# Queries and keys first in the projection, and the setup of a fused transformer block in another order

## The chip, the cores and the metric

One core of a Trainium2 chip runs the whole kernel in one launch. The metric is the device time of a launch in microseconds. TensorE (PE in the profile) multiplies matrices, VectorE (DVE), ScalarE (ACT) and GpSimd (POOL) do the elementwise work, and SyncE (SP) issues most of the DMAs. Each engine works through its own list of instructions in order and meets the others only in semaphores.

## The reference, cut to what matters

```python
mod = silu(condition) @ Wada + bada                       # (8, 6*512)
sh_a, sc_a, gt_a, sh_m, sc_m, gt_m = split(mod, 6)
xm = layernorm(x, g1, be1) * (1 + sc_a) + sh_a            # x is (8, 1024, 512), f32
q, k, v = heads(xm @ Wqkv)                                # 16 heads of 32
attn = softmax(causal(q @ k.T * 32**-0.5))
x = x + gt_a * ((attn @ v) @ Wproj + bproj)
xm = layernorm(x, g2, be2) * (1 + sc_m) + sh_m
x = x + gt_m * (gelu(xm @ W1 + b1) @ W2 + b2)             # hidden width 2048
```

## The kernel before, in words

Products with weights are made from a high and a low part of each operand (three matmuls for one), so each weight and each activation is split: ScalarE or VectorE rounds it to the high part, VectorE or GpSimd subtracts to get the low part.

**The projection** (Wqkv) runs over 16 blocks of 512 rows of x. A block (`ia`) is normalised on VectorE (`ln_stats`, `ln_aggregate`, `normalise`, the power on GpSimd), turned by four PE transposes (`a_turn`), given scale and shift on ScalarE (`a_modulate`), split on VectorE (`a_split`, one column part k at a time) and then multiplied in 12 items (`a_item`) of 12 matmuls each. Items 0 to 3 are the values of 128 rows each, items 4 to 7 the queries of a group of four heads, items 8 to 11 the keys. ScalarE copies each item out of PSUM (`a_copy`); a value item goes to DRAM from ScalarE's own queue (`v_store`); a query or key item is split by a cast on VectorE (`a_high`) and a subtraction on GpSimd (`a_low`), and SyncE stores it (`a_store`).

**Attention** runs over 32 pairs of batch and head group, two in each of 16 bodies of 40 steps. In each step PE makes scores, ScalarE takes their exponentials, GpSimd masks and adds, and PE multiplies by the values. A row's largest score is found beforehand: nine pieces for each pair (`max_item`), each some wide matmuls into psS (line 745), on VectorE a mask where the piece meets the diagonal (line 1223) and a reduction (line 1227). PE may begin piece n only when piece n-1 has been reduced, since both lie in psS. `max_join`, `max_turn` and `max_row` make a row of the results, and `place_max` sets it beside the queries.

**What runs ahead.** Blocks 0, 1 and 2 are projected in the setup, before body 0 (AHEAD = 3); body u projects block u+3 in its steps by the written table `A_SHARES`, and works on the largest scores of later pairs by `MAX_AT`. The setup has the nine pieces of pair 0 behind items 1 to 9 of block 2; the pieces of pair 1 stand in body 0, the first six in its first six steps (`MAX_FIRST_AT`). Where a step ends an item, the step after has its `a_high`, the next its `a_store`.

**The start.** The modulation is made from silu(condition) and six parts of Wada of 1 MB each: parts 0 and 1 ahead of block 0, parts 2 to 5 between blocks 0 and 1. Each part is four fp32 matmuls of eight output rows by 512 columns (line 672), all into PSUM partitions 0 to 7, followed by four small transposes (line 679). VectorE makes the coefficients from them (lines 1153, 1156). Wqkv is loaded and split in four row parts of 128x1536; VectorE makes the low parts of two of them (line 1136), GpSimd those of the other two, and item 0 needs all four.

**The end of attention.** Behind the last body SyncE issues the loads of six of the eight parts of W2, then waits for the stores of the attention's output and only then issues `load_x_gate(1)`, which brings gate, biases and x rows for block 1 of the MLP, and after it the attended rows of block 2.

The whole order is written out by hand; no planner moves anything.

## Time and profile before

| | us |
|---|---|
| median of three runs | 3336.97 (3336.56 to 3337.72) |
| profiled execution, its own time | 3334.65 |
| its span | 3332.9 |
| PE busy | 3207.0 |
| DVE busy | 2081.0 |
| POOL busy | 1549.8 |
| ACT busy | 1175.2 |
| mean granted clock of TensorE | 0.993 |

The span is what the profile covers; the execution's own time is 1.75 us more. Busy times of the engines overlap, so they don't add to the span. Times in the rows below count from the span's start. From there on the setup ends and body 0 begins at 176, attention ends near 1683, and the MLP takes the rest.

### The profile page before, as it was taken

The numbers are of one execution on the slowest core, as the hardware profiler recorded it, in microseconds if no ns is written. First come the engines' busy times: TensorE is split into PE (matmuls) and PEld (weight loads), VectorE is DVE, ScalarE is ACT, GpSimd is POOL, SyncE is SP. The second block draws the span as 40 slices with busy tenths as digits, with TensorE's granted clock in tenths as the row PEclk, the third lists the DMA queues.
The fourth block names the chain that finished last, engine by engine and source line by source line (L and its number), as shares of the span: only waits on it lengthen the run. The fifth ranks groups of instructions, "written<-read, shape, count | busy, mean of one in ns | idle before, by whom it ended". The sixth has DMA issues, their size and how long they took to land.

```text
span 3332.9 us, 70516 instructions
## 1 busy us (share of the span) xinstructions
PE 3207.0 (96%) x25708; PEld 2575.1 (77%) x25708; DVE 2081.0 (62%) x2511; ACT 1175.2 (35%) x2330; POOL 1549.8 (47%) x1304
## 2 busy tenths in 40 slices
PE   7989999999999999998889999999999999999999
PEld 4656666666666666665578898898988989889888
DVE  5567777677777767667665555555555555555552
ACT  2245555555555555555531121211211212112111
POOL 2246666666666666677762332333333333323232
PEclk9989999999999999999999999999999999999999
DMA  5546656656565665566632222222122222222220
GB/s 216 186 131 176 184 169 172 180 166 176 176 184 168 172 180 167 163 191 170 153 108 61 71 53 60 72 57 60 53 63 72 53 60 69 60 60 53 60 63 13
DMA packets 303514, 391.88 MB, mean 118 GB/s; under 512 B 24240, under 2 KB 206000, under 8 KB 303336
## 3 DMA queue, kind: packets, MB, share of 16 engines
q1 hardware_dynamic: 292080, 372.04, 39.6%
q10 hardware_dynamic: 11264, 17.31, 1.5%
q8 instruction: 140, 2.29, 0.3%
q14 instruction: 30, 0.25, 0.0%
HBM read 270.66 MB, written 118.06 MB: 117 GB/s over the span
## 4 chain that ended last, share of the span: by engine, by line
PE 85%; DVE 8%; issue 3%; ACT 2%; DMA 1%; SPq 0%; DVEq 0%; POOL 0%; ACTq 0%
PE psH L920 21%; PE psY L933 21%; PE psA L729 10%; PE psT L770 7%; PE psA L807 6%; PE psP L830 5%; PE psA L725 4%; DVE mx L1227 4%; PE psS L745 4%; PE psA L780 3%; DVE psS L1223 2%; DVE xm_h L1201 1%; PE psA L698 1%; PE psP L840 1%; PE psT L672 1%
## 5 line engine op out<-in xcount | busy, mean ns | idle before, releaser
L1474 POOL TENSOR_TENSOR h_l<-h_full,h_h 128x256 fp32r<-128x256 f32 x512 | 488.8, 955 | 1105.0 <-DVE h_h L1394 1105.0
L998 ACT ACTIVATE e<-psT 128x512 f32<-128x512 f32 (+1 forms) x1202 | 605.2, 554 | 596.6 <-PE psT L770 595.1
L1514 POOL TENSOR_TENSOR es<-e 128x1024 f32<-128x1024 f32 (+1 forms) x320 | 625.4, 1954 | 391.4 <-PE psA L780 218.5
L1227 DVE TENSOR_REDUCE mx<-psS 128x4 f32<-128x2048 f32 (+3 forms) x384 | 666.1, 1756 | 212.6 <-PE psS L745 205.6
L1102 ACT ACTIVATE h_full<-psH,b1c 128x256 f32<-128x256 f32 x512 | 243.6, 476 | 1316.4 <-PE psH L920 1316.4
L920 PE MATMUL psH<-a_l,w1p_h 128*128 128x256 f32 x2048 | 576.0, 281 | 0.0
L920 PE MATMUL psH<-a_h,w1p_l 128*128 128x256 f32 x2048 | 576.0, 281 | 0.0
L920 PE MATMUL psH<-a_h,w1p_h 128*128 128x256 f32 x2048 | 574.1, 280 | 0.0
L1394 DVE CAST h_h<-h_full 128x256 fp32r<-128x256 f32 x512 | 156.4, 306 | 521.9 <-ACT h_full L1102 520.9
L770 PEld LDWEIGHTS psT<-qst,kst 97*128 97x128 f32 x2404 | 353.6, 191 | 119.4 <-issue 70.8
L770 PE MATMUL psT<-qst,kst 97*128 97x256 f32 (+1 forms) x2404 | 410.1, 290 | 14.2 <-ACT e L998 12.2
L920 PEld LDWEIGHTS psH<-a_l,w1p_h 128*128 128x128 f32 x2048 | 387.7, 189 | 21.7
L933 PE MATMUL psY<-w_h,h_h 128*128 128x512 f32 x1024 | 404.3, 395 | 0.0
L933 PE MATMUL psY<-w_l,h_h 128*128 128x512 f32 x1024 | 403.9, 394 | 0.0
L920 PEld LDWEIGHTS psH<-a_h,w1p_h 128*128 128x128 f32 x2048 | 387.1, 189 | 21.6 <-issue 0.2
L933 PE MATMUL psY<-w_h,h_l 128*128 128x512 f32 x1024 | 402.5, 393 | 0.0
L920 PEld LDWEIGHTS psH<-a_h,w1p_l 128*128 128x128 f32 x2048 | 388.3, 190 | 0.0
L1316 DVE RECIPROCAL oin<-oin 128x256 f32<-128x256 f32 x128 | 222.7, 1743 | 173.1 <-DMA oin<-sums 173.1
L807 PE MATMUL psA<-e,vst 128*32 128x256 f32 (+1 forms) x5120 | 315.1, 364 | 4.7 <-ACT o_sb L1006 4.0
L1223 DVE TENSOR_TENSOR psS<-psS,mask_q 128x1024 f32<-128x1024 f32 (+1 forms) x160 | 162.9, 1018 | 173.6 <-PE psS L745 173.6
L1487 POOL TENSOR_TENSOR qk_hl<-qk_hl 128x512 fp32r<-128x512 f32 x128 | 172.9, 1351 | 171.0 <-DVE qk_hl L1210 171.0
L807 PEld LDWEIGHTS psA<-e,vst 128*32 128x32 f32 x5120 | 155.2, 110 | 123.1 <-issue 36.8
(113 smaller groups left out, 4751.8 us busy)
## 6 DMA issues: line engine op xcount, KB each, us to landing
qk_split<-qk_hl SPq DMA_DIRECT2D x128, 512.0 KB, 3.4
kst<-qk_split SPq DMA_DIRECT2D x128, 256.0 KB, 4.1
qst<-qk_split SPq DMA_DIRECT2D x128, 256.0 KB, 4.2
xin<-in_x_dram SPq DMA_DIRECT2D x64, 256.0 KB, 4.0
values<-vout ACTq DMA_DIRECT2D x64, 256.0 KB, 3.5
kmx<-qk_split SPq DMA_DIRECT2D x32, 512.0 KB, 4.6
qmx<-qk_split SPq DMA_DIRECT2D x32, 512.0 KB, 5.8
kst<-qk_split SPq DMA_DIRECT2D x128, 128.0 KB, 3.9
```

The costliest lines, as they stand in the source:

```text
L729: mm = pe.matmul(psA[:, bank, :], w[:, k, m * P:(m + 1) * P], a[:, k, :], **ends)
L770: mm = pe.matmul(bank[:, d, 0:w], kst[0:97, hd, key_cols(kt, h)], qst[0:97, q0 // HALF, hd, q0 % HALF:q0 % HALF + w], start=True, stop=Tru ...
L807: mm = pe.matmul(psO[HD * hd:HD * (hd + 1), c:c + w], vst[:, h, kt, HD * hd:HD * (hd + 1)], e[:, (2 * t + d) % ERING, hd, 0:w], start=(kt ...
L920: mm = pe.matmul(psH[:, m % 4, 0:RA], w[:, k, m * P:(m + 1) * P], a[par][:, k, :], start=(n == 0), stop=(n == 3 * KT - 1))
L933: mm = pe.matmul(psY[:, r, :], a[:, m % 4, r * P:(r + 1) * P], w[:, w2_at(m), :], start=(m == 0 and n == 0), stop=(m == FT - 1 and n == 2) ...
L998: act.activation(e[:, s % ERING, 2 * hp:2 * hp + 2, 0:w], score_bank(s, hp, with_a)[:, :, 0:w], ACT.Exp, scale=SCALE).then_inc(sem("exp_do ...
L1102: act.activation(h_full[:, m % 4, :], psH[:, m % 4, 0:RA], ACT.Gelu, bias=b1c[:, m:m + 1])\
L1223: dve.tensor_tensor(at, at, mask_q[:].to_broadcast([P, GH, len(chunks), P]), ALU.add)\
L1227: reduce = dve.tensor_reduce(mx[:, part, :, qt], psS[:, :, col:col + w], AX_X, ALU.max)
L1316: dve.reciprocal(oin[:, 1, k], oin[:, 1, k]).then_inc(sem("sums_inverted"), 1)
L1474: return pool.tensor_tensor(dst, full, high.bitcast(F32), ALU.subtract)
L1514: pool.tensor_tensor(to, first, second, ALU.add).then_inc(sem("added"), 1)
```

## The change

Items 0 to 7 of a block are now the queries and keys, in turn, of head groups 0 to 3, and items 8 to 11 are the values. This holds for the blocks of the setup and for those projected in the bodies. The first two items of block 1 complete all that pair 0 needs of batch 0, so `load_max(0, 0)` stands behind the second store of block 1.

In the setup:

- The nine pieces of pair 0 stand behind items 5 to 10 of block 1 and 0, 1 and 3 of block 2; the first three pieces of pair 1 stand behind items 6, 8 and 10 of block 2. `max_join`, `max_turn` and `max_row` of pair 0 stand at item 5 of block 2. Body 0 has the same table as the others.
- The cast of a query or key item in the setup is on ScalarE (`a_high_alone`), no longer on VectorE.
- The condition is turned before silu, so silu works on 128 partitions by 32 and is in place. Parts 0 and 1 of Wada are loaded ahead of x, the other four behind block 1's x. The matmuls of modulation write four groups of PSUM partitions (0, 32, 64, 96): parts 0 and 1 as halves of 256 columns, parts 2 to 5 as one group each. Of the six results the four that become coefficients are turned, in two `mod_turn`s; parts 2 to 5 are multiplied behind item 7 of block 0. Only the two gates are stored to DRAM.
- Wqkv is loaded and split in three column parts of 512: queries, keys, values. VectorE makes the low parts of the first two, GpSimd that of the third. Item 0 waits for the first, item 1 for the second, item 8 for the third.
- The small loads and bada are issued by ScalarE; the memset of a row of kst moves from VectorE to GpSimd.
- SyncE's order in the setup follows the new items. Behind the last body `load_x_gate(1)` is issued after two of the six remaining parts of W2.

The core of the diff:

```diff
-A_NV, A_NQK = 4, 8
-A_ITEMS = A_NV + A_NQK
+
+A_NQK, A_NV = 8, 4
+A_ITEMS = A_NQK + A_NV
...
-MAX_FIRST_AT = dict(enumerate([(1, n) for n in range(6)])) | {7: (1, 6), 9: (1, 7), 11: (1, 8)}
+
+MAX_ALONE_AT = {(1, 5): (0, 0), (1, 6): (0, 1), (1, 7): (0, 2), (1, 8): (0, 3), (1, 9): (0, 4), (1, 10): (0, 5),
+                (2, 0): (0, 6), (2, 1): (0, 7), (2, 3): (0, 8), (2, 6): (1, 0), (2, 8): (1, 1), (2, 10): (1, 2)}
+TURN_ALONE_AT, PLACE_ALONE_AT = (2, 5), (2, 7)
+
+
+MOD_FORM_AT, MOD_TURN_AT = 7, 9
...
-            bada_sb = sb(setup, "bada_sb", [B, 6, D])
-            mod = sb(setup, "mod", [B, 6, D])
-            csb = sb(setup, "csb", [B, 4, D])
+            bada_sb = sb(setup, "bada_sb", [P, 2, D])
+            mod = sb(setup, "mod", [P, 2, D])
+            csb = sb(setup, "csb", [B, D])
+            silu = sb(setup, "silu", [P, 3, KT * B])
...
-            sp.dma_start(csb[:, 0], cond).then_inc(sem("cond_loaded"), 16)
-            sp.dma_start(bada_sb[:], bada.rearrange("(n d) -> n d", n=6).partition_broadcast(B))\
-              .then_inc(sem("bada_loaded"), 16)
-            for n, v in enumerate((g1, be1, g2, be2)):
-                sp.dma_start(gb[:, n], v).then_inc(sem("small_loaded"), 16)
-            sp.dma_start(b1c[:], b1).then_inc(sem("small_loaded"), 16)
+            sp.dma_start(csb[:], cond).then_inc(sem("cond_loaded"), 16)
+            for n in range(2):
+                sp.dma_start(wada[:, n], wa_v[:, :, n * D:(n + 1) * D]).then_inc(sem(f"wada_loaded{n}"), 16)
...
-            for n in range(6):
+            for c in range(3):
+                sp.dma_start(wqkv[:, :, c * D:(c + 1) * D], wq_v[:, :, c * D:(c + 1) * D])\
+                  .then_inc(sem(f"wqkv_loaded{c}"), 16)
+            for r in range(NXR):
+                load_x(1, r)
+            for n in range(2, 6):
                 sp.dma_start(wada[:, n], wa_v[:, :, n * D:(n + 1) * D]).then_inc(sem(f"wada_loaded{n}"), 16)
-                if n == 1:
-                    for k in range(KT):
-                        sp.dma_start(wqkv[:, k], wq_v[:, k]).then_inc(sem(f"wqkv_loaded{k}"), 16)
-
...
+                if isinstance(u, int) and u == 0 and ahead < 2:
+                    own = {2 * hg + kind: 2 + 1 for kind in (Q, K)}
+                else:
+                    own = dict.fromkeys(range(QK_RING), (b + 1) * (2 * A_NQK // QK_RING))
+                for s, stores in own.items():
+                    sp.wait_ge(qk_stored[s], stores * 16)
...
+            for n in range(A_NQK):
+                a_store(0, n)
+                if n == 5:
+                    for r in range(NXR):
+                        load_x(2, r)
+            store_gates()
+            sp.wait_ge(sem("cond_turned"), 1)
+            for n in range(A_NQK):
+                a_store(1, n)
+                if n in (1, 3):
+                    load_max(0, n // 2)
+                if n == 5:
+                    for r in range(NXR):
+                        load_x(3, r)
...
+            for n in range(2):
+                a_store(AHEAD - 1, n)
+            sp.wait_ge(sem("mod_stored"), 32)
+            sp.wait_ge(sem("mod_turned"), 2)
...
+            for n in range(W2_EARLY, W2_PIECES // 2):
+                w2_load(n)
+            load_x_gate(1)
...
+                for n in range(first, end):
+                    pe.wait_ge(sem(f"wada_loaded{n}"), 16)
+                jobs = [(n, half) for n in range(first, end) for half in range(2)] if first == 0 else \
+                    [(n, None) for n in range(first, end)]
+                for k in range(KT):
+                    for n, half in jobs:
+                        at, part, c = mod_place(n, half or 0)
+                        cols = slice(0, D) if half is None else slice(256 * half, 256 * (half + 1))
+                        w = cols.stop - cols.start
+                        mm = pe.matmul(psT[at:at + B, part, c:c + w], sT[:, k, :], wada[:, n, k, cols],
+                                       start=(k == 0), stop=(k == KT - 1), skip_group_check=True)
+                mm.then_inc(sem("mod_formed"), 1)
+
+            def mod_turn(shift, scale, ready):
+                pe.wait_ge(sem("mod_ready"), ready)
+                for n in (shift, scale):
+                    for k in range(KT):
+                        at, part, first = mod_place(n, k // 2)
+                        mm = pe.transpose(mod_turned(n, k), mod[at:at + B, part, first + k % 2 * P:first + (k % 2 + 1) * P],
+                                          ident[at:at + B, at:at + B])
+                mm.then_inc(sem("mod_turned"), 1)
 
             modulation(0, 2)
...
+                    if n < A_NQK:
+                        m = n % 2 * IPB + n // 2
                         a, w = ((xm_h, wqkv_h), (xm_l, wqkv_h), (xm_h, wqkv_l))[q % 3]
                         mm = pe.matmul(psA[:, bank, :], w[:, k, m * P:(m + 1) * P], a[:, k, :], **ends)
+                    else:
+                        m = n - A_NQK
+                        a, w = ((xm_h, wqkv_h), (xm_h, wqkv_l), (xm_l, wqkv_h))[q % 3]
+                        mm = pe.matmul(psA[:, bank, :], a[:, k, m * P:(m + 1) * P], w[:, k, 2 * D:3 * D], **ends)
                     if n == A_ITEMS - 1 and q % 3 == 2 and k < KT - 1:
...
+                    if ia == 0 and n < 2:
+                        pe.wait_ge(sem("wqkv_lo"), n + 1)
+                    if ia == 0 and n == A_NQK:
+                        pe.wait_ge(sem("wqkv_lo_pool"), KT)
                     a_item(ia, n, 0, A_MM, True, False)
-                    if ia == AHEAD - 1:
-                        if n == 0:
-                            pe.wait_ge(sem("coef_ready"), 2)
-                        if 0 < n <= NMX:
-                            max_item(0, 0, n - 1)
+                    if (ia, n) == (0, MOD_FORM_AT):
+                        modulation(2, 6)
+                    if (ia, n) == (0, MOD_TURN_AT):
+                        mod_turn(3, 4, 8)
+                    if (ia, n) in MAX_ALONE_AT:
+                        ahead, piece = MAX_ALONE_AT[ia, n]
+                        if (ahead, piece) == (0, 0):
+                            pe.wait_ge(sem("coef_ready"), 2 * KT)
+                        max_item(0, ahead, piece)
+                    if (ia, n) == TURN_ALONE_AT:
...
+            def wqkv_high(c):
+                act.wait_ge(sem(f"wqkv_loaded{c}"), 16)
+                cols = slice(c * D, (c + 1) * D)
+                act.activation(wqkv_h[:, :, cols], wqkv[:, :, cols], ACT.Copy).then_inc(sem("wqkv_hi"), 1)
+
+            def a_high_alone(ia, n):
+
+                act.wait_ge(sem("a_copied"), ia * A_ITEMS + n + 1)
+                act.activation(qk_hl[:, n % QK_RING, HIGH[n % 2]].bitcast(F32R), qk_hl[:, n % QK_RING, LOW[n % 2]],
+                               ACT.Copy).then_inc(sem("qk_hi"), 1)
+
...
+            wqkv_high(0)
+            act.wait_ge(sem("coef_ready"), KT)
             for k in range(A_TURNS):
                 a_modulate(0, k, True)
...
+            for c in (1, 2):
+                wqkv_high(c)
             for ia in range(AHEAD):
                 for n in range(A_ITEMS):
                     a_copy(ia, n, True)
-                    if 0 < n <= A_NV:
+                    if n < A_NQK:
+                        a_high_alone(ia, n)
+                    if n > A_NQK:
                         v_store(ia, n - 1)
                     if n in TURN_AFTER_ALONE:
                         a_modulate(ia + 1, TURN_AFTER_ALONE.index(n), True)
-            place_max(0, 0, 1)
+                    if (ia, n) == PLACE_ALONE_AT:
+                        place_max(0, 0, 1)
...
+            def modulation(part, w):
+                dve.wait_ge(sem(f"bada_loaded{part}"), 4 * 16)
+                dve.wait_ge(sem("mod_formed"), part + 1)
+                for at in range(0, P, 32):
+                    dve.tensor_tensor(mod[at:at + B, part, 0:w], psT[at:at + B, part, 0:w], bada_sb[at:at + B, part, 0:w],
+                                      ALU.add).then_inc(sem("mod_ready"), 1)
...
+                if ia == 0:
+                    modulation(0, 256)
...
             layer_norm(0)
-            modulation(0, 1)
-            wqkv_low(0)
-            modulation(1, 2)
             dve.wait_ge(sem("small_loaded"), 5 * 16)
             coefficients(0, 0, 1)
-            wqkv_low(2)
+            wqkv_low(0)
             for k in range(KT):
                 a_split(0, k)
+            wqkv_low(1)
+            dve.wait_ge(sem("mx_set"), 1)
+            dve.wait_ge(sem("masks_ready"), 1)
             for ia in range(AHEAD):
-                if ia == 1:
-                    modulation(2, 6)
-                    coefficients(1, 3, 4)
                 for n in range(A_ITEMS):
+                    if (ia, n) in MAX_ALONE_AT:
+                        max_item(0, *MAX_ALONE_AT[ia, n])
+                    if (ia, n) == TURN_ALONE_AT:
+                        max_join(0, 0)
+                        max_row(0, 0)
                     if n == 3 and ia < AHEAD - 1:
                         layer_norm(ia + 1)
-                    if n == 0 and ia == AHEAD - 1:
+                    if (ia, n) == (0, MOD_FORM_AT + 1):
+                        modulation(1, D)
+                    if (ia, n) == (1, 0):
+                        coefficients(1, 3, 4)
+                    if (ia, n) == (AHEAD - 1, 2):
+                        for r in range(NXR):
+                            ln_stats(AHEAD, r)
+                        ln_aggregate(AHEAD)
+                    if (ia, n) == (AHEAD - 1, 4):
                         for r in range(NXR):
                             normalise(AHEAD, r)
                     if n == A_ITEMS - 1:
                         for k in range(KT - 1):
                             a_split(ia + 1, k)
-                    a_high(ia, n)
-                    if ia == AHEAD - 1:
-                        if n == 0:
-                            dve.wait_ge(sem("mx_set"), 1)
-                            dve.wait_ge(sem("masks_ready"), 1)
-                        if 0 < n <= NMX:
-                            max_item(0, 0, n - 1)
                 a_split(ia + 1, KT - 1)
-                if ia == AHEAD - 2:
-                    for r in range(NXR):
-                        ln_stats(AHEAD, r)
...
+            pool.wait_ge(sem("wqkv_hi"), 3)
+            for k in range(KT):
+                low(wqkv_l[:, k, 2 * D:3 * D], wqkv[:, k, 2 * D:3 * D], wqkv_h[:, k, 2 * D:3 * D])\
+                    .then_inc(sem("wqkv_lo_pool"), 1)
```

## Rows read from the trace of the kernel before

**Rows 1.** The page's first part: busy us, share, instructions.
```profile
PE 3207.0 (96%) x25708; PEld 2575.1 (77%) x25708; DVE 2081.0 (62%) x2511; ACT 1175.2 (35%) x2330; POOL 1549.8 (47%) x1304
```

**Rows 2.** The chain that ended last, 0 to 400: start, us, what.
```profile
5.81 7.21 DMA wada<-in_L_cond_Wada_dram
...
13.16 9.54 PE psT L672 x16
...
25.39 4.57 DVE wqkv_l L1136
31.16 13.09 PE psA L725 x48
...
70.17 6.96 PE psT L672 x16
...
86.06 11.10 PE psA L725 x48
...
176.39 2.71 PE psA L725 x6
```

**Rows 3.** Waits of PE, 0 to 400: total us, times, longest.
```profile
PE psS L745 <- DVE mx L1227: 13.2, 12, 2.0
...
PE psA L725 <- DVE xm_l L1203: 5.0, 2, 3.6
PE psS L752 <- DVE mxc L1234: 4.4, 1, 4.4
```

**Rows 4.** Stretches, PE: stretch, length, busy (instructions), clock, DMA share, GB/s.
```profile
175.00:180.00 5.00, 3.11 (x7) 0.52 0.70 194
```

**Rows 5.** Instructions in order of time, 0 to 60: start, us, engine, line.
```profile
10.94 2.45 DVE L1163 BATCH_NORM_STATS2 stats<-xin 128x6 f32<-128x512 f32 x4
...
17.57 1.48 ACT L1075 ACTIVATE wqkv_h<-wqkv_full 128x1536 fp32r<-128x1536 f32 x1 [5.62 <-DMA wqkv_full<-in_L_cond_Wqkv_dram]
...
19.89 1.73 DVE L1136 TENSOR_TENSOR wqkv_l<-wqkv_full,wqkv_h 128x1536 fp32r<-128x1536 f32 x1
...
21.02 7.32 POOL L1474 TENSOR_TENSOR wqkv_l<-wqkv_full,wqkv_h 128x1536 fp32r<-128x1536 f32 x2 [5.99 <-ACT wqkv_h L1075]
```

**Rows 6.** Stretches, loads of weights: stretch, length, clock, DMA share, GB/s.
```profile
14.00:16.00 2.00, 1.00 1.03 419
```

**Rows 7.** PE in order of time, beginning of body 1.
```profile
286.41 0.74 PE L770 MATMUL psT<-qst,kst 97*128 97x256 f32 x4
...
295.48 1.07 PE L807 MATMUL psA<-e,vst 128*32 128x256 f32 x16
```

**Rows 8.** Groups by shape, 0 to 180: busy us, mean ns of one.
```profile
L1227 DVE TENSOR_REDUCE mx<-psS 128x4 f32<-128x2048 f32 x6 | 13.7, 2291 | 2.0 <-PE psS L745 2.0
...
L1144 DVE TENSOR_TENSOR mod<-psT,bada_sb 8x512 f32<-8x512 f32 x6 | 4.1, 678 | 12.0 <-PE psT L672 12.0
...
L1223 DVE TENSOR_TENSOR psS<-psS,mask_q 128x1024 f32<-128x1024 f32 x3 | 3.7, 1225 | 0.0
...
L745 PE MATMUL psS<-kmx,qmx 32*128 32x512 f32 x24 | 3.0, 494 | 4.4 <-DVE mx L1227 4.4
```

**Rows 9.** ACT in order of time: `a_modulate` of step 23, bodies 0 and 1.
```profile
244.74 0.78 ACT L976 ACTIVATE xin<-psA,coef 128x512 f32<-128x512 f32 x1
...
342.06 0.78 ACT L976 ACTIVATE xin<-psA,coef 128x512 f32<-128x512 f32 x1 [0.26 <-PE psA L698]
```

**Rows 10.** PE in order of time, a largest score's piece in a later body's first steps.
```profile
484.45 0.56 PE L745 MATMUL psS<-kmx,qmx 32*128 32x128 f32 x8 [1.22 <-DVE mx L1227]
```

**Rows 11.** DVE in order of time, the cast of a query or key item.
```profile
471.54 1.17 DVE L1210 CAST qk_hl<-qk_hl 128x512 fp32r<-128x512 f32 x1
```

**Rows 12.** DMA issues, 95 to 180: KB each, median us to landing.
```profile
qk_split<-qk_hl SPq DMA_DIRECT2D x16, 512.0 KB, 3.5
...
kmx<-qk_split SPq DMA_DIRECT2D x2, 512.0 KB, 6.2
```

**Rows 13.** Waits of PE, 1600 to the end: total us, times, longest.
```profile
PE psP L840 <- DVE xc L1370: 5.2, 1, 5.2
```

More of the change, by code:

```diff
@@ L153, in item_ended, with mod_place @@
     return at[0] if at and at[2] == A_MM and at[1] < A_MM else None
-def max_at(u, h):
-    if isinstance(u, int) and u == 0 and h == 0:
-        return MAX_FIRST_AT | {r: piece for r, piece in MAX_AT.items() if piece[0] == 2}
-    return MAX_AT
+def mod_place(n, half):
+    return (32 * (2 * n + half), 0, 0) if n < 2 else (32 * (n - 2), 1, 256 * half)
 def wait(eng, sem, value):
@@ L329, in w2_piece, with mod_turned @@
             return t[:, w2_at(2 * n):w2_at(2 * n) + 2, :]
+        def mod_turned(n, k):
+            at = mod_place(n, k // 2)[0]
+            return psS[:, at // 32, k * B:(k + 1) * B]
         def past(eng, name):
@@ L505, in _ @@
                 load_q(0, 0, p)
-            load_max(0, 1)
+            for n in range(2):
+                a_store(AHEAD - 1, n)
+            sp.wait_ge(sem("mod_stored"), 32)
+            sp.wait_ge(sem("mod_turned"), 2)
             load_v(0, 0)
-            for n in range(A_NV, A_ITEMS):
+            for n in range(2, A_NQK):
                 a_store(AHEAD - 1, n)
@@ L610, in body @@
                     item = ended(u, s - A_STORE_LAG, with_a, after_a)
-                    if item and item[1] >= A_NV:
+                    if item and item[1] < A_NQK:
                         a_store(*item)
@@ L634, in _ @@
             sp.wait_ge(sem("pv_done"), NIT * SLOTS)
-            for n in range(W2_EARLY, W2_PIECES):
+            for n in range(W2_EARLY, W2_PIECES // 2):
+                w2_load(n)
+            load_x_gate(1)
+            for n in range(W2_PIECES // 2, W2_PIECES):
                 w2_load(n)
@@ L664, in _ @@
-            pe.wait_ge(sem("cond_copied"), 1)
             def modulation(first, end):
-                for n in range(first, end + 1):
-                    if n < end:
-                        pe.wait_ge(sem(f"wada_loaded{n}"), 16)
-                        wait(pe, sem("mod_ready"), n - 1)
-                        for k in range(KT):
-                            mm = pe.matmul(psT[0:B, n % 2, :], sT[:, k, :], wada[:, n, k, :],
-                                           start=(k == 0), stop=(k == KT - 1))
-                        mm.then_inc(sem("mod_formed"), 1)
-                    if n > first:
-                        pe.wait_ge(sem("mod_ready"), n)
-                        for k in range(KT):
-                            c = ((n - 1) * KT + k) * B
-                            mm = pe.transpose(psS[:, int(n > 2), c:c + B], mod[:, n - 1, k * P:(k + 1) * P], ident[0:B, 0:B])
-                        mm.then_inc(sem("mod_turned"), 1)
+                for n in range(first, end):
+                    pe.wait_ge(sem(f"wada_loaded{n}"), 16)
@@ L1058, in body @@
                             o_copy(u, h - back, n)
-                    if with_a and item_ended(s - 1) is not None and item_ended(s - 1) < A_NV:
-                        v_store(u + AHEAD, item_ended(s - 1))
+                    item = ended(u, s - 1, with_a, after_a)
+                    if item and item[1] >= A_NQK:
+                        v_store(*item)
                     if r in PLACE_AT and not (last and h + PLACE_AT[r][0] == 2):
@@ L1131, in _ @@
             dve.wait_ge(sem("silu_step"), 2)
[L1132 to L1145 removed]
+            dve.tensor_tensor(sT[:].rearrange("p k b -> p (k b)"), psA[:, 0, 0:KT * B], silu[:, 1], ALU.mult)\
+               .then_inc(sem("silu_ready"), 1)
```

160 lines of the change are left out of this document (65 added, 95 removed).

## The prediction

> **What bounds the kernel now.** I read the page's busy times first [rows 1]: PE is busy for 3207.0 of 3332.9 us, no other engine for two thirds. So time comes only out of what PE waits for, out of work that PE needn't do, and out of work done at half clock. The chain of waits over the first 400 us [rows 2] then shows where the setup isn't PE's own: the first projection matmul comes only at 31.2, behind a load of Wada that lands at 13.0, modulation matmuls to 22.7 and a VectorE split; and between blocks 0 and 1 PE spends 70.2 to 86.1 on modulation. The waits of PE in the same stretch [rows 3] name what is left: 13.2 us on the reductions of the largest scores, 4.4 on the join, 5.0 on the splits of xm. The clock in the stretch where body 0 begins [rows 4] is 0.52 on average, so mostly the lower level, 1.2 GHz; PE had waited 4.4 us for the join just ahead. Everything from body 1 on I take from two anchors in ScalarE's order of time [rows 9].
>
> **The start: about -8.5.** The first Wada part landed 13.0 with 1 MB of x ahead of it, issued at 5.8 [rows 2]. Now it is issued at about 1.3 and both parts must be there; the second has the same 1 MB ahead of it that x was. 4.5 us earlier gives 8.5; the small loads run beside it and the first issue has a start-up, so I take 10.3. The matmuls on it: 8 of 512 columns took 9.5 us, part of it at low clock [rows 2]. In four column groups the same columns pass four at a time. That these overlap the trace shows in the values' matmuls, 16 instructions of 256 columns on 32 output columns each in 1.07 us [rows 7]; full-width fp32 takes 6.96 us for 16 instructions of 512, so 3.5 for as many columns [rows 2]: a factor of 3.3. At half clock I get 3.4 us, done at 13.8, against 9.5. x lands after the two parts: 1 MB at 419 GB/s [rows 6] is 2.5 us, 12.9, its statistics end near 13.3, as before (10.94 + 2.45 [rows 5]). Then the power (1 us), four additions of at most 0.68 each [rows 8], taken as 0.4 for half the columns, and four normalisations (1.9): 17.5. Coefficients 1.8: 19.3. VectorE's low part of the queries' Wqkv is 1.73 x 4/3 = 2.3 [rows 5] and GpSimd is idle: 21.6. The first split 1.1 (the power, normalisations, coefficients and splits are read in the same order of time as rows 5): item 0 at 22.8 instead of 31.2. Silu, now 32 columns wide, is done by 6.5, under the load. Bounds: 20 (x earlier) to 26 (the lines above each 1 us late).
>
> **Block 0: about -10.5.** Before, 31.2 to 86.1 is 54.9 us, of which 39.0 are the twelve items and 15.9 the modulation with its turns and additions. The items without the low clock at their beginning are 37.0 (11.10 for four [rows 2], three turns and their waits). Now: item 0 is paced by the splits and by the low clock, 5.5 instead of 2.8 (+2.7). Item 1 needs the keys' low part: VectorE begins it at 25.9, after the last split, and ends 28.3, which is what item 0's end plus 0.8 already holds. The modulation of parts 2 to 5 is 32 instructions of 512 columns, 13.9 us by rows 2 at 6.96 for 16; in four groups 3.6, plus eight turns, 0.8. Sum 37.0 + 2.7 + 4.4 = 44.1. Bounds of the modulation: 3.5 and 13.9, the nearest row [rows 7] speaks for the low end. A wait on its loads is not due: 5 MB issued from 17.5 are in by 32, and PE wants them at 47.
>
> Here a port matters. One VectorE low part took 1.73 us and the next, made while GpSimd was at its two (7.32 for both), 4.65 [rows 5]. The cause that I read in it is that VectorE stood until GpSimd's instruction ended. Now GpSimd makes its four parts of 512 columns (1.2 each) when ScalarE has rounded the third column part, near 26.4; VectorE has begun the keys at 25.9. I take no loss; if GpSimd is first, item 1 waits from 1.2 to 4.9 more.
> The Trainium skill (SBUF — State Buffer, "SBUF: two separate sides") says that whichever of the two engines starts first holds the shared ports for its whole instruction and the other blocks. By that rule the cost is none or a full GpSimd instruction, nothing between. The 4.65 agrees with it.
>
> **Blocks 1 and 2: about -6.** Before, 86.1 to 176.4 is 90.3 [rows 2]. Now two clean blocks, 74.0, plus twelve pieces at 0.5 on PE [rows 8], 6.0, and one turn, 0.4. A piece with a full mask holds psS for 0.5 + 1.2 + 2.3 = 4.0 us [rows 8]; an item and its piece give it 3.2, an item with a turn 3.9, so three pieces wait, 0.8 together. The casts, now on ScalarE (0.6 us beside 1.4 of other work per item of 2.7), are hidden, and VectorE has them no more. Splits at the end of a block: 0.2 at the first, where no reduction stands ahead; 2.1 at the second, where VectorE is 3.5 us in piece 5 of pair 0 (before: 1.4 of wait and a thin item, the same). The new wait is for `load_max(0, 0)`: SyncE stands until the stores of items 0 and 1 have landed, and behind it are the stores of items 2 and 3, whose slots ScalarE wants back only four items later. From item 1's end: copy and cast on ScalarE 0.6 each, GpSimd 1.3 and the hops, 2.7; store 3.5; issue and load 6.2 and 0.4 [rows 12]: 12.8. PE asks after four items, 10.9. Those latencies come from a busier stretch, so I take 1.0 of wait, bounds 0 and 3. Sum 84.5: -5.8. The join's 4.4 [rows 3] is gone, since items stand behind it; late next is the exchange of psS, priced above.
>
> **Body 0: about -14.** Body 1 begins at 286.4 [rows 7] and needs 55.7 to its step 23 (342.06 [rows 9]). Body 0 began at 176.4 and needed 68.3 to the same point (244.74). The 12.7 are six pieces in its first six steps with one reduction each on VectorE, the wait for `place_max` and the low clock [rows 3, 4]. With the table of the others it needs 55.7 less the one group of values and two sums of a body before that it hasn't, 1.5. So 68.3 - 54.2 = 14.1. The three pieces that go from here to block 2 are counted there.
>
> **Bodies 1 to 12: about -4.5.** PE's work is the same. VectorE's casts and GpSimd's subtractions of four items move from a body's second half to its first. At a body's beginning PE waits 1.2 us [rows 10] for piece 2, late behind the splits, with GpSimd in their way; the items ending there are now values. A cast there took 1.17 [rows 11]. Bounds a body: -1.5 (both waits there vanish), and in the first half, where the nine pieces share VectorE with normalisation, up to +1.2 for one cast in four that hits a piece. I take -0.4, x 12.
>
> **Behind the last body: about -3.** PE waits 5.2 once, for x rows of block 1 of the MLP [rows 13]. Gate and x rows are now issued about 10 us earlier. What is late next is the attended rows of block 2, behind the same wait on stores; VectorE inverts them ahead of the normalisation. That gives back about 2. Bounds 0 and 5.2.
>
> **Sum.** -8.4 - 10.8 - 5.8 - 14.1 - 4.5 - 3 = -46.6 on the profiled execution's 3334.65: 3288. The median is 2.3 above that execution (1.75 of it lies around the span in both), so 3290.
>
> **The rivals.**
> - *The column groups don't overlap in the modulation* (8 output rows are no full group; rows 7 have 32). Then 13.9 instead of 3.6, and 6 more at the start, part of it under x: +14, 3304. Chance 0.08.
> - *The setup's chain of stores and loads sets the pace*: `load_max` 3 us late, pieces 1 us late each, VectorE behind GpSimd at item 1: +12, 3302. For it: 6.2 us of landing; against: few loads in block 1. Chance 0.12.
> - *The relief at the bodies' beginnings is whole*: -1.5 x 12 = -18 instead of -4.5: 3277. For it: the cast's 1.17. Chance 0.12.
> - *The first half of the bodies gets slower*, by 0.8 a body: +14, 3304. Chance 0.12.
> - *It ends slower*: the four casts moved into the first half of each body each delay a piece by their full 1.17 and the four subtractions of GpSimd delay its sums by as much. Two thirds of 4 x 2.4 is 6.4 a body, x 12 = 77, against 42 of the rest: 3372. It decides from 3.5 us a body. Against it: VectorE is idle in several places between those pieces. Chance 0.02.
> - *The change doesn't do what it says*: something later in the setup (a slot of the ring, a load of x) holds PE until the old time. Less than 7 us off the whole: 3330. Chance 0.02.
>
> **How the numbers follow.** The forecast, 3282 to 3298, has 0.52. The range takes in the fast rival and the three at 3302 to 3304 with their spread: 3275 to 3309. Faster by over 0.2% (6.7 us, about what a measurement of this kernel can tell) 0.97, within 0.2% 0.01, slower 0.02.
>
> **What would show it.** The first projection matmul at 22 to 24; modulation after item 7 near 4 us; body 0's matmuls at about 151 and at the higher clock from its first step; `a_modulate` of step 23 of body 1 near 303 instead of 342, 97 or a little less to the next; the wait on `xc` behind the last body under 3. Wrong if PE waits for the loads of qmx and kmx for more than 3 us, if psT's modulation takes over 10, or if a body's period is over 97.5.

## The result, and the profile after

| | before | after |
|---|---|---|
| median | 3336.76 (3336.28 to 3337.72) | 3312.82 (3305.70 to 3316.73) |
| span of the profiled execution | 3332.9 | 3311.4 |
| PE busy | 3207.0 | 3205.5 |
| mean granted clock | 0.993 | 0.991 |

The ratio of after to before is 0.9925 (95%: 0.9908 to 0.9943). The change takes 24 us off, where 47 were forecast with a range of 28 to 62 us. So it is faster, but by half of what was said.

The setup came out as forecast. The kernel after, instructions in order of time (start, us, engine, line):

```profile
13.68 0.69 DVE L1223 BATCH_NORM_STATS2 stats<-xin 128x6 f32<-128x512 f32 x1 [0.32 <-DMA xin<-in_x_dram]
...
20.08 2.28 DVE L1198 TENSOR_TENSOR wqkv_l<-wqkv_full,wqkv_h 128x2048 fp32r<-128x2048 f32 x1
...
23.57 0.77 PE L754 MATMUL psA<-xm_h,wqkv_h 128*128 128x512 f32 x1 [0.57 <-DVE xm_l L1265]
...
26.53 2.29 DVE L1198 TENSOR_TENSOR wqkv_l<-wqkv_full,wqkv_h 128x2048 fp32r<-128x2048 f32 x1
27.49 6.24 POOL L1535 TENSOR_TENSOR wqkv_l<-wqkv_full,wqkv_h 128x512 fp32r<-128x512 f32 x4 [11.41 <-ACT wqkv_h L1122]
...
48.13 3.62 PE L696 MATMUL psT<-wada,sT 128*8 128x512 f32 x32
...
84.36 0.51 PE L774 MATMUL psS<-kmx,qmx 32*128 32x512 f32 x4 [1.17 <-DMA qmx<-qk_split]
...
151.69 0.47 PE L754 MATMUL psA<-xm_h,wqkv_h 128*128 128x512 f32 x1 [0.95 <-ACT vout L1033]
```

The first projection matmul is at 23.57 (31.16 in [rows 2]), the late modulation (parts 2 to 5) takes 3.62 us for its 32 instructions, where 16 of these took 6.96 before [rows 2], `load_max` makes PE wait 1.17 us, and body 0 begins at 151.69 instead of 176.39.

What follows is read from the anchor of [rows 9], `a_modulate` of step 23, which comes once in a body; from one anchor to the next is a body's period. Bodies 0, 1, 2, 3 and 11:

```profile
206.19 0.78 ACT L1020 ACTIVATE xin<-psA,coef 128x512 f32<-128x512 f32 x1
301.66 0.78 ACT L1020 ACTIVATE xin<-psA,coef 128x512 f32<-128x512 f32 x1 [0.27 <-PE psA L726]
398.69 0.78 ACT L1020 ACTIVATE xin<-psA,coef 128x512 f32<-128x512 f32 x1 [0.26 <-PE psA L726]
497.57 0.78 ACT L1020 ACTIVATE xin<-psA,coef 128x512 f32<-128x512 f32 x1 [0.26 <-PE psA L726]
...
1286.33 0.78 ACT L1020 ACTIVATE xin<-psA,coef 128x512 f32<-128x512 f32 x1 [0.26 <-PE psA L726]
```

From body 0 to 1 it is 95.47 us, to body 2 97.03, and from then on 98.6 to 98.9 (the last 97.4). Before, every body took 97.2. So the first body after the change is 1.9 us shorter and most of the others are 1.6 us longer. In ScalarE's order of time the later bodies have a hole (idle time) at their beginning, here that of body 3:

```profile
443.23 1.09 ACT L1042 ACTIVATE e<-psT 128x512 f32<-128x512 f32 x2 [4.47 <-issue]
```

"issue" means that ScalarE waited for nothing that the profile shows. It stands where ScalarE's loop over bodies 1 to 11 (`Fori`) returns to its first instruction, ten times, for 4.07 to 4.47 us; the first hole ends at 345.82. PE stands behind it, and in eight of the ten the clock goes down in the time after. PE in order of time, then stretches of PE (stretch, length, busy and instructions, clock, DMA share, GB/s):

```profile
443.88 1.20 PE L799 MATMUL psT<-qst,kst 97*128 97x256 f32 x4 [1.65 <-ACT e L1042]
```

```profile
442.00:444.00 2.00, 0.35 (x3) 1.00 0.24 74
444.00:446.00 2.00, 2.00 (x16) 0.62 0.35 135
446.00:448.00 2.00, 2.00 (x32) 0.52 0.21 72
448.00:450.00 2.00, 2.00 (x14) 1.00 0.63 178
```

PE is busy for all of 444 to 448, and the clock there is 0.62 and 0.52 on average, mostly the lower level of 1.2 GHz. That loses about (0.38 + 0.48) x 2 = 1.7 us, with the wait of 1.65 about 3.4 us a return, and 98.7 less 95.24, the period that the experiments below give without the hole, is 3.5. At the first return and at the last the clock stayed at 1.00. The last two periods, as stretches of PE:

```profile
1090.33:1188.92 98.59, 95.81 (x966) 0.98 0.60 173
1188.92:1286.33 97.41, 94.27 (x966) 1.00 0.59 174
```

PE waited 1.29 us at the return of the one and 1.65 at that of the other. The eight periods with the clock at 0.98 are 98.8 us long in the mean with PE busy for 95.7 to 95.8; the two at 1.00 are 97.03 and 97.41 with 94.3. So the low clock costs 1.5 us where it comes, and the hole without it about 2.

The page has one line that changed with it: the queue that brings ScalarE's instructions (queue, packets, MB, share).

```profile
q14 instruction: 81, 0.66, 0.1%
```

Before it was 30 packets. PE's busy time fell by 1.5 us only; in e10 below, the same kernel without the holes, it is 3182.5, 23 us less, since matmuls at the lower level count longer.

### The profile page after: what moved, and what is told of

It is laid out like the page before. It is cut to its first block, busy times and chain, and to the rows that moved or that the text cites. A ratio compares the mean times of both kernels' runs of the same rounds, so it can differ in the third digit from the quotient of the medians.

```text
span 3311.4 us, 70585 instructions
## 1 busy us (share of the span) xinstructions
PE 3205.5 (97%) x25716; PEld 2580.2 (78%) x25716; DVE 2032.7 (61%) x2494; ACT 1189.2 (36%) x2352; POOL 1551.3 (47%) x1307
## 3 DMA queue, kind: packets, MB, share of 16 engines
q8 instruction: 140, 2.29, 0.3%
## 4 chain that ended last, share of the span: by engine, by line
PE 89%; DVE 5%; issue 2%; ACT 2%; DMA 1%; SPq 1%; POOL 0%; ACTq 0%; DVEq 0%
PE psH L953 22%; PE psY L966 21%; PE psA L754 10%; PE psT L799 8%; PE psA L836 7%; PE psA L758 5%; PE psP L859 5%; PE psS L774 4%; PE psA L809 3%; DVE mx L1287 2%; DVE psS L1283 1%; PE psA L726 1%; PE psP L869 1%; ACT e L1042 1%; PE psA L846 1%
## 5 line engine op out<-in xcount | busy, mean ns | idle before, releaser
L966 PEld LDWEIGHTS psY<-w_h,h_l 128*128 128x128 f32 x1024 | 192.4, 188 | 42.5
```

The lines of the kernel that those rows point to most:

```text
L966: mm = pe.matmul(psY[:, r, :], a[:, m % 4, r * P:(r + 1) * P], w[:, w2_at(m), :], start=(m == 0 and n == 0), stop=(m == FT - 1 and n == 2) ...
```

## The experiments

**Theory A.** ScalarE holds two adjacent blocks of its instructions. Its loop is just over one block long; in the kernel after it lies in three blocks, so that at every return code must be fetched. Its rival, theory B, is that the new order of the loop's instructions makes the hole. The Trainium skill (Runtime: NRT & Kernel Launch, "Instruction fetch mechanics") says that most engines hold two blocks of 256 instructions, filled in sequence, and that a taken branch out of these two stalls until the target is fetched. The positions of the loop were counted in the traces: ScalarE's instructions in the order in which it executed them, the first as number 0 (the recorded 304 counts from 1).

**e1_pad16**: the kernel after, its loop moved by 16 instructions. They count up a semaphore that nobody waits for.

```diff
+            for _ in range(16):
+                act.sem_inc(sem("pad"), 1)
             wqkv_high(0)
```

> The changed kernel with 16 semaphore increments more on ScalarE, at a place of the setup where it idles, so that its loop over bodies 1 to 11 begins 16 instructions later. Nothing else differs. In the changed kernel ScalarE stands 4.1 to 4.5 us at each return of that loop, and the profile shows about four instruction packets of queue 14 there, none in the kernel before. Theory A, the loop's code came to lie so that a return finds its beginning no longer held and has it fetched: 16 instructions further it lies well again; the holes and some 50 packets are gone, a body's period falls from 98.7 to about 95.5, the time from 3313 to about 3278. Theory B, the content of the loop (values stored in the first step of the body behind): nothing changes, 3313 and 98.7.

Measured: 3276.23 (3271.09 to 3277.15), ratio 0.9810 (0.9794 to 0.9827). The anchors stand at

```profile
300.57 0.78 ACT L1020 ACTIVATE xin<-psA,coef 128x512 f32<-128x512 f32 x1 [0.27 <-PE psA L726]
...
395.81 0.78 ACT L1020 ACTIVATE xin<-psA,coef 128x512 f32<-128x512 f32 x1 [0.26 <-PE psA L726]
```

a period of 95.2 in all bodies 1 to 11. The page has 31 packets for the queue, and at the loop's returns no ScalarE hole of over 3 us is left. Sixteen instructions that do nothing give 37 us.

**e2_unroll**: the kernel after with ScalarE's bodies 1 to 11 written out.

```diff
-            with act.Fori(1, NU - AHEAD - 1) as u:
+            for u in range(1, NU - AHEAD - 1):
```

> The changed kernel with ScalarE's bodies 1 to 11 written out instead of looped. Theory A (a return of the loop fetches code): no return, no hole, period about 95.5, about 3278. Theory B (the store in the first step costs by itself): the hole stays at the beginning of each body, 3305 to 3313. A third outcome: straight code must be fetched too, and if that were slow the exponentials would be late all over, above 3313.

Measured: 3276.59 (3274.48 to 3280.80), ratio 0.9820 (0.9804 to 0.9837), period 95.25, 42 packets. Without a return there is no hole, and 11 more packets that came in sequence cost nothing that shows.

**e3_before_pad33**: the kernel before with 33 such instructions.

```diff
+            for _ in range(33):
+                act.sem_inc(sem("pad"), 1)
```

> The kernel before with 33 semaphore increments more on ScalarE in its setup, so that its loop begins at the instruction at which that of the changed kernel begins (304). Item order and setup are those of before. Theory A: the hole of 4 us and the packets of queue 14 appear at each return here too; PE waits for the exponentials 1.2 to 1.7 us instead of partly for the reduction, and the clock may fall after it; period 97.2 to 98 or 100, time 3342 to 3367. Theory B: nothing appears, 3337.

Measured: 3340.05 (3336.90 to 3343.78), ratio 1.0005 (0.9996 to 1.0015), period 97.17, 31 packets. The expected hole did not come. The count offers a reason: the loop before has 272 instructions and its first round now ended at number 574, that of after (273) at 575. So either one instruction decides, or the hole belongs to the new order. The next two tell.

**e5_pad15**: e1 with one instruction less ahead of the loop.

```diff
-            for _ in range(16):
+            for _ in range(15):
```

> The changed kernel with 15 increments of an unused semaphore on ScalarE ahead of the rounding of Wqkv, where e1_pad16 had 16. Theory A (ScalarE holds two adjacent blocks of 256 of its own executed instructions; its loop of 273 instructions now begins at executed instruction 318, one short of the boundary at 319, and so lies in three blocks): the hole of about 4 us at each return of ScalarE's loop is there again, 4 instruction packets per return (about 80 in all), a period of 98.7, and 3313 us (3305 to 3318), not 3276. Rival (the padding helped by something coarser, a shift in time or the start's order): one instruction less changes nothing, 31 packets, period 95.2, 3276.

Measured: 3332.26 (3328.57 to 3336.88), ratio 0.9981 (0.9971 to 0.9990), 82 packets. One instruction costs 56 us. The hole is there again, and longer than in the kernel after, where the same waits of PE are 18.1, 22 times, 1.6 the longest: ScalarE in order of time, then waits of PE 400 to 1500 (total us, times, longest).

```profile
448.90 1.09 ACT L1042 ACTIVATE e<-psT 128x512 f32<-128x512 f32 x2 [5.45 <-issue]
```

```profile
PE psT L799 <- ACT e L1042: 29.1, 18, 3.4
```

Theory A in its direction, wrong in its size (3313). The trace's single instructions show the second part of the price. Executed number and start of each on ScalarE at the first return (counted out of the trace, not a view):

```
e5:    590 branch 341.1    591 at 344.9    592 at 347.5    (then 0.1 apart)
after: 575 branch 341.5    576 at 345.6    577 at 345.7    (then 0.1 apart)
```

By the count below, the loop's first instruction in e5 is the last one of its block, so two fetches of 3.8 and 2.6 us stand in a row. In the kernel after 16 instructions of the loop lie before the boundary, and I take it that the second fetch goes on beside them: neither they nor the one behind them starts late.

**e6_before_pad40**: the kernel before with 40 instead of 33.

> The kernel before with 40 such increments on ScalarE, so that its loop of 272 runs from about executed instruction 310 to 581 and crosses the boundary at 575 (with 33 it ended at 574, and nothing happened). Theory A: the kernel before gets the same hole, 4 us at each of 11 returns, about 80 instruction packets instead of 30, a period above 97.6 instead of 97.2, and 3342 to 3367 us. The rise may be smaller than in the changed kernel, since at its bodies' beginnings PE waited already and part of the hole lies beneath that. Rival (the hole belongs to the new order of instructions in a body, not to where the loop lies): 3337 to 3340, 31 packets, period 97.2.

Measured: 3350.54 (3348.53 to 3352.45), ratio 1.0035 (1.0021 to 1.0049), 81 packets, a period of 98.4 in the mean. The kernel before gets the hole as well:

```profile
484.06 1.09 ACT L998 ACTIVATE e<-psT 128x512 f32<-128x512 f32 x2 [4.23 <-issue]
```

So the hole doesn't belong to the new order. There are ten of them, one at each return (the expectation's 11 is a miscount), and they cost less here, 1.2 us a body, where PE waits at the bodies' beginnings without them too. All positions of ScalarE's first round of the loop, in executed instructions:

```
kernel   loop        length  lies in blocks      period
before   270 to 541  272     63-318, 319-574     97.18
e3       303 to 574  272     63-318, 319-574     97.17
e6       310 to 581  272     three               98.4
after    303 to 575  273     three               98.5
e5       318 to 590  273     three              101.0
e1       319 to 591  273     319-574, 575-830    95.23
```

The boundaries 319 and 575 were found by single steps: 318 against 319 at the beginning (e5, e1, the same kernel), 574 against 575 at the end (e3, after, which are two kernels; in the kernel before itself it is 574 against 581). They lie 256 apart (the 63 and the 830 are worked out with that), which agrees with the block that the Trainium skill gives in the section named above.

**e4_tail_back** and **e9_pad16_tail_back**: `load_x_gate(1)` behind all parts of W2, as before, in the kernel after and in e1.

```diff
-            for n in range(W2_EARLY, W2_PIECES // 2):
-                w2_load(n)
-            load_x_gate(1)
-            for n in range(W2_PIECES // 2, W2_PIECES):
+            for n in range(W2_EARLY, W2_PIECES):
                 w2_load(n)
             o_store(NU - 1, 1, 3)
...
+            load_x_gate(1)
```

> The changed kernel with the load of gate, biases and x rows for block 1 of the MLP issued again after all parts of W2, as before. The prediction had this step at -3; from the end of attention on the changed kernel is 3.5 us slower than the kernel before, with a new wait of 2.7 us for h_l. If the moved load does that, this kernel is faster by about 3 (3310) and the wait for h_l is gone, while the one of 5.2 stays; if the step brings what was forecast and something else costs it, this kernel is slower by about 3 (3316).

> e1_pad16 with load_x_gate(1) issued behind all six parts of W2, as in the kernel before, so that this step is measured without the holes of ScalarE's loop. If the step gives the 3 us that the prediction put on it: 3279, with the wait on xc at 5 again. If it gives nothing, because the wait for the attended rows or for VectorE's inversion is what ends last (the changed kernel's wait on xc was 5.2 all the same, with one of 2.7 on h_l ahead of it): the same as e1_pad16 to 1 us, 3275 to 3277.

**e10_pad16_again**: e1 once more, on the chip of e9.

> The kernel of e1_pad16 word for word, as the yardstick on the same chip: 3276 (3274 to 3278), ratio 0.981 to 0.982.

Measured: e4 3311.96 (3308.84 to 3315.03), ratio 0.9926 (0.9909 to 0.9942), the same as after. e9 3274.06 (3272.31 to 3275.71) and e10 3274.01 (3272.49 to 3277.78), ratios 0.9807 and 0.9808. So the step gives nothing, as the second expectation of e9 had it; of e4's two, 3 us faster and 3 us slower, neither came. Waits of PE from 1600 on, first e9, then e10:

```profile
PE psP L867 <- DVE xc L1427: 5.3, 1, 5.3
```

```profile
PE psP L869 <- DVE xc L1429: 4.8, 1, 4.8
```

The chain of waits of e10 shows what ends last (start, us, what):

```profile
1627.14 1.08 SPq L591
1628.34 0.71 SPq L437
1629.09 9.62 DMA sums<-o_sb
...
1641.13 5.83 DMA oin<-sums
```

It isn't x or the gate but the attended rows (`oin`), which wait for the last store of attention. That store (L437) goes out 3.0 us later than in e9, where it is at 1625.29; four more loads (gate, two biases, x) stand ahead of it on SyncE.

**e12_store_first**: that store ahead of the loads.

```diff
             sp.wait_ge(sem("pv_done"), NIT * SLOTS)
+            o_store(NU - 1, 1, 3)
             for n in range(W2_EARLY, W2_PIECES // 2):
...
-            o_store(NU - 1, 1, 3)
```

> e10_pad16_again with the last store of attention's output issued ahead of the six remaining parts of W2 and of load_x_gate(1). In e10 the copy that it stores ends at 1622.2, but SyncE issues it only at 1628.3, behind those loads; the attended rows of block 2 are asked for when it has landed (1638.7) and come at 1647, and PE waits 4.8 for xc. Theory (this store is what ends last there, so that load_x_gate(1) could give nothing by being early): the store goes out at 1622.5, the attended rows come 5 to 6 us earlier, the wait on xc is below 1, and the time is 3269 to 3271, 4 to 5 below e10. Rival: the loads of W2 that now begin 1.2 us later are wanted at once by ScalarE and PE waits on psY or psH instead: 3273 to 3276.

Measured: 3275.48 (3270.70 to 3276.74), ratio 0.9805 (0.9792 to 0.9819): no gain, and the wait on xc is 5.2. That is the rival's time, but not its cause: PE has no wait on psY or psH. The store went out at 1623.6, and from the last anchor on that is 5.9 us earlier than in e10. But the chain of e12 now reads

```profile
1635.62 1.90 SPq L536
1637.56 1.32 SPq L536
1638.92 10.19 DMA oin<-sums
```

and its stretches

```profile
1630.00:1635.00 5.00, 5.00 (x34) 1.00 1.00 263
1635.00:1640.00 5.00, 5.00 (x28) 1.00 1.05 390
1640.00:1645.00 5.00, 5.00 (x28) 1.00 0.94 205
```

The DMA engines are full (shares of 0.94 to 1.05) with six parts of W2 of 512 KB each, and the rows asked for earlier land no earlier. My theory of SyncE's order fell. What I read in its place, that the amount to be moved before 1649 ends last there, is not shown; loading some of W2 later was not tried.

**e7_body_order_back**: e1 with the items of the bodies in the order of before, the setup as changed.

```diff
+def item_kind(n, alone):
+    if alone:
+        return n < A_NQK, n if n < A_NQK else n - A_NQK
+    return n >= A_NV, n - A_NV if n >= A_NV else n
...
-                if n < A_NQK:
+                qk, i = item_kind(n, False)
+                if qk:
```

> e1_pad16 with the items of the bodies in the order of before (values 0 to 3, then queries, then keys); the setup stays changed, and ScalarE's loop lies in two blocks. Theory: the relief of 1.9 us a body comes from the order of the items, so the period is 97.2 again and the time 3276 + 12 x 1.94 = 3299 (3294 to 3303); the wait of PE for piece 2 of a body (psS, 1.2 us) is back. Rival: the relief comes from something that stays (the setup's state, where the pieces stand in time): period 95.2, 3276.

Measured: 3299.93 (3297.31 to 3302.03), ratio 0.9881 (0.9864 to 0.9897), period 97.17, as expected. The item order alone is worth 1.93 us a body. VectorE, GpSimd and PE at the beginning of body 2 in e7, and then in e1:

```profile
341.46 1.29 POOL L1587 TENSOR_TENSOR es<-e 128x512 f32<-128x512 f32 x1 [0.26 <-POOL e L1569]
341.82 1.22 DVE L1274 CAST xm_h<-xin 128x512 fp32r<-128x512 f32 x1
342.70 1.86 POOL L1569 TENSOR_SCALAR_AFFINE_SELECT e<-e 128x512 f32<-128x512 f32 x2
...
343.07 1.00 DVE L1276 TENSOR_TENSOR xm_l<-xin,xm_h 128x512 fp32r<-128x512 f32 x1
...
344.00 0.85 DVE L1274 CAST xm_h<-xin 128x512 fp32r<-128x512 f32 x1
...
344.83 1.28 POOL L1587 TENSOR_TENSOR es<-e 128x512 f32<-128x512 f32 x1 [0.26 <-POOL e L1569]
344.88 1.78 DVE L1276 TENSOR_TENSOR xm_l<-xin,xm_h 128x512 fp32r<-128x512 f32 x1
346.59 2.28 DVE L1299 TENSOR_REDUCE mx<-psS 128x4 f32<-128x2048 f32 x1
...
348.92 0.56 PE L782 MATMUL psS<-kmx,qmx 32*128 32x128 f32 x8 [1.23 <-DVE mx L1299]
```

```profile
338.70 0.42 DVE L1265 CAST xm_h<-xin 128x512 fp32r<-128x512 f32 x1
339.15 0.69 DVE L1267 TENSOR_TENSOR xm_l<-xin,xm_h 128x512 fp32r<-128x512 f32 x1
...
339.76 0.86 DVE L1265 CAST xm_h<-xin 128x512 fp32r<-128x512 f32 x1
...
340.65 1.00 DVE L1267 TENSOR_TENSOR xm_l<-xin,xm_h 128x512 fp32r<-128x512 f32 x1
341.36 1.42 POOL L1576 TENSOR_TENSOR es<-e 128x512 f32<-128x512 f32 x1 [0.26 <-POOL e L1558]
341.57 2.28 DVE L1289 TENSOR_REDUCE mx<-psS 128x4 f32<-128x2048 f32 x1
```

The same two casts and two subtractions of `a_split` take VectorE 1.22 + 1.00 + 0.85 + 1.78 = 4.85 us in e7 and 0.42 + 0.69 + 0.86 + 1.00 = 2.97 in e1, 1.88 less, near the 1.93 of the period. PE's waits on these reductions, between 400 and 1500, fall from 22.6 us in e7 to 6.5 in e1, 1.4 a body. So most of the 1.93 is seen on PE; that the stretched splits make it is read from body 2, not tested. The cast of 1.22 and the subtraction of 1.78 overlap a GpSimd instruction and end with it or behind it; in e1 GpSimd's addition falls beside the reduction, which it doesn't lengthen.

**e8_order_back_act** and **e11_new_order_act**: the casts of query and key items in the bodies on ScalarE, with the old order (e8, from e7) and with the new one (e11, from e1, whose edit is shown).

```diff
+                    if item and item[1] < A_NQK:
+                        i = item[1]
+                        act.wait_ge(sem("a_copied"), item[0] * A_ITEMS + item[1] + 1)
+                        past(act, "act")
+                        act.activation(qk_hl[:, i % QK_RING, HIGH[i % 2]].bitcast(F32R), qk_hl[:, i % QK_RING, LOW[i % 2]],
+                                       ACT.Copy).then_inc(sem("qk_hi"), 1)
...
-                    if item:
-                        a_high(*item)
```

> e7 with the casts of query and key items in the bodies on ScalarE and no longer on VectorE. It tells which of the two helpers at a body's beginning made the wait. If it is VectorE's time (cast 1.17 us ahead of the reduction): the wait goes, period 95.2, 3276. If it is GpSimd's subtraction, which holds what VectorE needs or comes late for the next: 97.2 as in e7, 3299. ScalarE has 8 casts of 0.6 us more a body and is 35% busy; should their place before its exponentials delay PE, up to 8 x 0.6 = 4.8 a body more, 3276 to 3330.

> e1_pad16 with the casts of query and key items in the bodies on ScalarE. With the old order of items this cost 3.2 us a body (e8 against e7): GpSimd's subtraction came earlier, its addition of es with it, and that stood in the way of VectorE's xm_l (2.75 instead of 0.69 us). Theory (the price comes from this meeting at a body's beginning): with the values there no item is cast near it, the meeting doesn't occur, and the time is 3270 to 3280. Rival (casts in ScalarE's order always hold up its exponentials or leave VectorE to run into GpSimd somewhere): 3285 or more.

Measured: e8 3335.53 (3331.67 to 3338.77), ratio 0.9990 (0.9980 to 1.0000), 36 us worse than e7 with less work on VectorE, and beyond all that the expectation had. It has 32 instruction packets and no hole. Its ten periods are 99.1 three times and 100.6 seven times, and what tells them apart is the clock. Stretches of PE:

```profile
609.18:708.25 99.07, 94.13 (x967) 1.00 0.60 172
708.25:808.82 100.57, 95.65 (x966) 0.98 0.58 169
```

Body 2's beginning in e8:

```profile
352.51 2.57 POOL L1591 TENSOR_TENSOR es<-e 128x1024 f32<-128x1024 f32 x1
352.87 2.75 DVE L1282 TENSOR_TENSOR xm_l<-xin,xm_h 128x512 fp32r<-128x512 f32 x1
...
359.21 0.80 PE L782 MATMUL psS<-kmx,qmx 32*128 32x512 f32 x4 [2.10 <-DVE mx L1305]
```

With the cast on ScalarE GpSimd has its subtraction earlier and begins its addition of 2.57 us just ahead of VectorE's last `xm_l`. That one needs 0.69 alone and ends 0.54 behind GpSimd, and the pieces behind it are late. PE's waits on the reductions, 400 to 1500, are 36.8 us against e7's 22.6. The Trainium skill (SBUF — State Buffer, "SBUF: two separate sides") says that the engine that starts first keeps the shared ports for its whole instruction; 2.75 for 0.69 agrees. e11 is 3277.35 (3276.43 to 3284.30), ratio 0.9816 (0.9803 to 0.9830), period 95.25, as its theory had it: with values at the bodies' beginnings the two don't meet, and e11 is neither better nor measurably worse than e10.

## Why the prediction was wrong

Terms on the profiled spans, in us; e10 is the kernel after without the hole:

| | forecast | after | e10 |
|---|---|---|---|
| to step 23 of body 0 | -39.1 | -38.6 | -39.7 |
| from there to step 23 of body 11 | -4.5 (with body 12) | +11.0 | -21.2 |
| the rest | -3 | +6.1 | +0.3 |
| sum | -46.6 | -21.5 | -60.6 |

- **The start** (-8.4): -7.6. x's last statistics end at 14.4 instead of 13.3, and the first matmul is at 23.57 instead of 22.8. Right.
- **Block 0** (-10.8): block 1 begins at 68.61, so 45.0 instead of 44.1, -9.9. The column groups overlap as [rows 7] had said: 3.62 against a forecast of 3.6. That rival is out. VectorE was first with the keys' low part (2.29, no loss) and GpSimd took 6.24 for its four: 2.47 for the first, which came while VectorE still had 1.3 to go, and 1.29 for each of the others. So "none or a full GpSimd instruction, nothing between" was wrong. As these durations read, the engine that comes second waits for the rest of the other's instruction: 1.2 us here, and in the 4.65 of [rows 5] 2.9 us of a GpSimd instruction of 3.4.
- **Blocks 1 and 2** (-5.8): 83.1 instead of 84.5, -7.2. `load_max` cost 1.17 where I had taken 1.0. The rival of stores and loads is out.
- **Body 0** (-14.1): 54.5 to its step 23, -13.85. Right.
- **Bodies 1 to 12** (-4.5): this is the step that failed, twice over. I named the relief at the bodies' beginnings and bounded it at -1.5, then took -0.4; e7 against e1 gives -1.93. It is the rival "the relief is whole", and past its bound of 1.5, which is near the 1.4 that PE's waits on the reductions give back; I had not counted by how much GpSimd stretches VectorE's splits there. And "PE's work is the same" was taken to mean that the other engines' loops cost the same as well. ScalarE's loop grew by one instruction and began 33 later, and each of ten returns then cost 3.2 us in the mean (98.47 against 95.25): 32 us that no term had. No rival named it. I had written that a period over 97.5 would show me wrong, and it was 98.7.
- **Behind the last body** (-3): the other step that failed. "What is late next is the attended rows" was right, but they take back all of the 5.2, not 2 of it: e9 and e10 are the same to 0.1 us. Of the +6.1 in the profiled execution of after, 2.7 is a wait on GpSimd's h_l that e10 doesn't have; the rest I can't place, and single executions spread there: e1 and e10, the same kernel, differ by 3.2, and e3 is 8.8 longer there than the kernel before, whose code it shares there.

The forecast of 3290 thus missed two things of opposite sign, 17 us of relief and 32 of fetching. That it is off by 23 us and not by more is luck: they partly cancel. Without the fetching the change is worth 64 us (3274.01 against 3338.38), more than the range allowed as well. That the code position is the cause is shown, in both directions and to one instruction. Of the 32 us the clock took 12 (1.5 at eight returns), read from periods of one trace with and without it; why it stayed up at two returns stays open.

## What to carry to other kernels

When a hardware loop on ScalarE has somewhat over 256 instructions (no run here tells of another engine's), its position is part of its cost: count the executed instructions ahead of it, and if the page's instruction packets grow or ScalarE shows a hole with "issue" at each return, shift the loop by a few idle instructions before judging a change. A change that adds one instruction to such a loop can lose more than all it was made for, so measure it with the loop in a good place too. And moving work off VectorE isn't a gain where it lets GpSimd start earlier on something that VectorE then stands behind.

## What the runs showed of the hardware

- What the runs fit is that ScalarE's code came in blocks of 256 instructions, held two at a time: boundaries at the executed numbers 319 and 575. A loop within two adjacent blocks fetched nothing in ten returns (before 1 packet in 350 to 1300, e1 none); one that touched three fetched 5 packets of 8 KB a round (loops of 272 and 273 instructions). DMA queues, 350 to 1300, kernel after:

```profile
q14 instruction: 46, 0.38, 0.2%
```

- One fetch at a return held ScalarE for 4.1 us (3.8 in e5), and where the next block was wanted at once, for 2.6 more. Crossing a boundary in sequence cost nothing visible (e2).
- The worst position of the same code (e5, 3332) and the best (e10, 3274) are 58 us apart, 1.7% of the kernel.
- A VectorE reduction out of PSUM kept its 2.28 us beside a GpSimd addition of 1.42, while a subtraction of two SBUF tiles went from 0.69 to 2.75 beside one of 2.57.
- A body's period was 1.5 us longer where the clock's mean in it was 0.98 instead of 1.00, in the kernel after as in e8.
